# Reordering the seam between two batches of an attention and expert kernel, and a seven step reciprocal square root

## The chip, the core and the metric

The kernel runs on one core of a Trainium2 chip. The metric is device time in microseconds (us), the median of several runs; a profiled execution of the same program gives the trace from which all rows below are taken. TensorE does the matrix products, VectorE, ScalarE and GpSimd the element work, and SyncE issues the transfers.

## The reference

The input is 8 sequences of 512 tokens, 256 features wide. Each goes through an attention block and an expert block:

```python
q, k, v = x @ Wq.T, x @ Wk.T, x @ Wv.T          # 32 heads of 8, rope on q and k
kmean = mean of k over chunks of 32 tokens
gate = einsum('bshd,bnhd->bhsn', q, kmean)      # future chunks out, own chunk in
sel = top 4 chunks of gate per token and head
p = softmax(where(allowed by sel and causal, q @ k.T / sqrt(8), -1e30))
o = p @ v
o = o * rsqrt(mean(o * o) + 1e-6) * o_norm_weight * sigmoid(x @ Wg1.T @ Wg2.T)
x = layernorm(x + o @ Wo.T)
# experts: 2 shared, 16 routed of width 176, top 4 of sigmoid(x @ centroids.T) + bias
x = layernorm(x + x + shared(x) + sum over experts of gate_e * (relu(x @ w1_e + b1_e) @ w2_e + b2_e))
```

## The kernel before, in words

The order of the work is written out by hand, one program for each engine, with semaphores between them. There are no planners; a step waits only where the code says so, and every engine works its list in order.

The work is pipelined over batches. Turn `b` does the attention of batch `b` and, woven between its steps on every engine, the experts of batch `m = b - 1`. The expert columns are cut into 25 chunks `c` of up to 128: `up` is the first product of a chunk (6 matmuls in 3 parts), then ScalarE's `relu` and `high`, GpSimd's `low` (the rest that half precision leaves), and `down`, the second product (12 matmuls). Tensors with a high and a low half-precision part stand for one 32-bit tensor.

A turn has these stages:

- Top-k: `stack` transposes keys and queries on TensorE; VectorE picks the chunks (`best`, `select`).
- Maxima: 40 `max_unit` products, each followed by a reduction on VectorE (L1314).
- Softmax: 8 groups of 4 heads. `key_unit` products (L498), ScalarE's exponentials (L973), GpSimd's causal masks (L1072, a burst of three for each group), and the products with `v` (`outputs`, L704). VectorE's `copy_outputs` (L1334) empties the product's bank, TensorE's `to_tokens` (L714) transposes it, and VectorE's `keep` (L1339) takes it back. Each two groups are normalised in `two_groups`: squares, sum, `root_guess` (a shift and a subtraction on the bits), three Newton steps of three instructions (L1140 to L1142), the product. After the first Newton step of such a pair stands the `copy_outputs` of the next group.
- Seam: the last group goes to tokens and through `two_groups`, `heads_out` and `project_out` (L753, L760) give the attention's output, `layernorm` makes `x1n`. Between these TensorE projects the next batch (`project_v` L395, `project_qk` L401) and ScalarE turns it (`turned`, the rope's products). Then the new turn starts: `rank_rows` (L416), `transpose_q` (L424), `chunk_means` (L432) for the first half of the tokens, `x1_transpose` (L507) once `x1n` is there, the second half, `router` (L518), the second `chunk_means`, `up` of chunk 0 (L552), `chunk_gates` (L443), `gate_rows` (L526, L529), `up` of chunk 1, `open_outputs` (L538), the first `down` (L564).

On VectorE the seam is the layernorm, the rope of the second half, `x1T_parts` (L1161, the low part of the transposed `x1n`), `route` (L1166 to L1185) with `block_diagonal` (L1221) in its middle, then `best`. `chunk_gates` on TensorE waits for `block_diagonal`, `gate_rows` waits for the end of `route`. On ScalarE it is `x1T_parts` (L846), `stack_high` of tile 2 (L870), the router's exponential (L850), the two copies of `qT` (L905), `stack_high` of tile 3. GpSimd's four products of the same tiles (L1045) follow `stack_high`, then `low` of chunk 0 (L1029).

## Time and profile before

| What | us |
|---|---|
| median of 3 runs | 1563.69 (1562.2 to 1566.65) |
| profiled execution, device time | 1564.33 |
| profiled execution, span | 1562.6 |
| TensorE busy | 1387.1 (89%) |
| VectorE busy | 1180.3 (76%) |
| ScalarE busy | 846.1 (54%) |
| GpSimd busy | 539.8 (35%) |
| mean granted clock of TensorE, share of full speed | 0.932 |

A turn takes some 184 us, and there are seven seams between turns. The seam after the fourth turn lies at 715 to 757 us of the span; the rows below are mostly from there. A timeline row gives start, duration, engine, line, operation, output and input, count, and in brackets the idle time before it with what ended it. PE is TensorE's matmul queue, DVE VectorE, ACT ScalarE, POOL GpSimd.

### The profile page before, as it was taken

To read this page: it belongs to the slowest core of one execution; us is meant where nothing else is said; L and a number is where in the kernel's file an instruction comes from. 1 tells how busy PE (TensorE), PEld (TensorE's weight loads), DVE (VectorE), ACT (ScalarE), POOL (GpSimd) and SP (SyncE) were. 2 spreads that over 40 slices of the span, in tenths; PEclk is the share of its full clock that TensorE was granted. 3 is DMA by queue.
4 is the path that set the end of the run, shared out by engine and by line. 5 is a ranking of instruction groups with operands and counts; after the bars stand their busy time and mean duration, and the time that the engine had idled before them with its cause. 6 is when DMAs were issued, how large, how long until landed. Compare 5 with 4: busy or idle time off the path is not lost.

```text
span 1562.6 us, 29670 instructions
## 1 busy us (share of the span) xinstructions
PE 1387.1 (89%) x11024; PEld 755.2 (48%) x11024; DVE 1180.3 (76%) x3027; ACT 846.1 (54%) x1266; POOL 539.8 (35%) x638
## 2 busy tenths in 40 slices
PE   5588899898998989989999899989899899999697
PEld 3322575435643466434654257544664346542364
DVE  7994778867786778967788777876789677885634
ACT  5408663385725765276642957348562776428221
POOL 4204432254323542244422543235322443224143
PEclk8758899998999989999999989999899999998799
DMA  6000021100221012111221002210112101220031
GB/s 239 8 15 8 28 76 64 39 29 29 76 68 35 15 56 75 48 29 29 69 68 43 19 24 82 68 30 28 49 62 68 29 15 61 71 48 15 14 103 60
DMA packets 52212, 77.83 MB, mean 50 GB/s; under 512 B 6322, under 2 KB 26724, under 8 KB 51812
## 3 DMA queue, kind: packets, MB, share of 16 engines
q1 hardware_dynamic: 52068, 75.94, 16.4%
q8 instruction: 87, 1.43, 0.4%
q14 instruction: 57, 0.47, 0.1%
HBM read 67.00 MB, written 8.65 MB: 48 GB/s over the span
## 4 chain that ended last, share of the span: by engine, by line
PE 52%; DVE 19%; issue 10%; ACT 9%; POOL 5%; DVEq 3%; DMA 1%; POOLq 1%; SPq 0%
PE PS L564 12%; PE PS L552 10%; PE PS L704 7%; POOL hp L1029 5%; PE PS L481 4%; DVE CM L1314 4%; ACT UQ L973 3%; PE PS L498 3%; ACT hp L834 3%; DVE hr L1125 2%; PE PS L714 2%; PE PS L760 2%; ACT UK L973 2%; PE PS L401 2%; PE PS L451 2%
## 5 line engine op out<-in xcount | busy, mean ns | idle before, releaser
L1029 POOL TENSOR_TENSOR hp<-hr,hp 128x512 f16<-128x512 f32 (+1 forms) x200 | 234.8, 1174 | 637.0 <-ACT hp L834 605.1
L1314 DVE TENSOR_REDUCE CM<-PS 128x32 f32<-128x1024 f32 x320 | 382.1, 1220 | 47.6 <-PE PS L481 45.1
L564 PE MATMUL PS<-W,hp 128*128 128x256 f16 (+1 forms) x2400 | 322.2, 278 | 26.5 <-POOL hp L1029 23.9
L552 PE MATMUL PS<-x1T,W 128*128 128x512 f16 (+1 forms) x1200 | 315.1, 390 | 0.0
L564 PEld LDWEIGHTS PS<-W,hp 128*128 128x128 f16 (+1 forms) x2400 | 216.4, 99 | 124.4 <-POOL hp L1029 65.0
L825 ACT ACTIVATE hr<-PS,CF 128x512 f32<-128x512 f32 (+1 forms) x200 | 137.3, 686 | 207.4 <-PE PS L552 195.8
L834 ACT ACTIVATE hp<-hr 128x512 f16<-128x512 f32 (+1 forms) x178 | 112.5, 632 | 227.7 <-DVE hr L1125 226.0
L1125 DVE TENSOR_TENSOR hr<-hr,gB 128x512 f32<-128x512 f32 x176 | 121.1, 688 | 84.5 <-ACT hr L825 81.2
L973 ACT ACTIVATE UK<-PS 128x1024 f32<-128x1024 f32 x160 | 152.8, 1036 | 29.0 <-PE PS L498 28.0
L552 PEld LDWEIGHTS PS<-x1T,W 128*128 128x128 f16 (+1 forms) x1200 | 108.8, 101 | 114.9 <-issue 39.7
L973 ACT ACTIVATE UQ<-PS 128x1024 f32<-128x1024 f32 x160 | 151.8, 1044 | 5.2 <-PE PS L498 3.4
L498 PE MATMUL PS<-qET,kz 64*128 64x512 f16 (+3 forms) x1024 | 114.6, 311 | 27.6 <-ACT UK L973 20.4
L1072 POOL TENSOR_SCALAR_AFFINE_SELECT UK<-UK 128x512 f32<-128x512 f32 x128 | 78.3, 636 | 165.8 <-ACT UK L973 165.8
L481 PE MATMUL PS<-kz,qET 64*128 64x512 f16 (+3 forms) x1024 | 132.2, 318 | 0.0
L498 PEld LDWEIGHTS PS<-qET,kz 64*128 64x128 f16 x1024 | 32.3, 95 | 174.8 <-ACT UK L973 78.9
L1072 POOL TENSOR_SCALAR_AFFINE_SELECT UQ<-UQ 128x512 f32<-128x512 f32 x128 | 79.2, 641 | 65.2 <-ACT UQ L973 65.2
L704 PE MATMUL PS<-UK,vst 128*9 128x512 f32 (+3 forms) x1024 | 94.5, 466 | 0.0
L704 PE MATMUL PS<-UQ,vst 128*9 128x512 f32 (+3 forms) x1024 | 83.9, 434 | 0.0
L1334 DVE COPY ropeb<-PS 128x512 f32<-128x512 f32 x64 | 44.2, 690 | 49.3 <-PE PS L704 47.3
L883 ACT ACTIVATE UK<-PS,CF 128x128 f32<-128x128 f32 x112 | 55.9, 511 | 44.4 <-PE PS L401 44.4
L1045 POOL TENSOR_TENSOR UQ<-UK,UQ 128x512 f16<-128x512 f32 x32 | 40.5, 1266 | 100.1 <-ACT UQ L870 99.9
L919 ACT ACTIVATE kz<-PS 128x1024 f16<-128x1024 f16 x64 | 65.2, 1018 | 14.0 <-PE PS L451 14.0
(151 smaller groups left out, 1959.4 us busy)
## 6 DMA issues: line engine op xcount, KB each, us to landing
gB<-gates SPq DMA_DIRECT2D x64, 256.0 KB, 3.2
gB<-gates SPq DMA_DIRECT2D x32, 224.0 KB, 2.8
gB<-gates SPq DMA_DIRECT2D x32, 192.0 KB, 2.8
gB<-gates SPq DMA_DIRECT2D x32, 160.0 KB, 2.5
xT<-in_xT SPq DMA_DIRECT2D x8, 512.0 KB, 3.7
qET<-rows SPq DMA_DIRECT2D x16, 256.0 KB, 5.8
v<-in_x SPq DMA_DIRECT2D x8, 512.0 KB, 4.1
gB<-gates SPq DMA_DIRECT2D x32, 128.0 KB, 2.8
```

The costliest lines, as they stand in the source:

```text
L481: mm = pe.matmul(PS[:, r + half, o:o + w], qET[rows, a, t * P:(t + 1) * P], kz[rows, a, 0:w], start=False, stop=True, skip_group_check=Tru ...
L498: mm = pe.matmul(PS[:, r + half, o:o + w], kz[rows, a, t * P:(t + 1) * P], qET[rows, a, t * P:S], start=True, stop=True, tile_position=(64 ...
L552: mm = pe.matmul(PS[0:w, BK_H[c % 2], :], W1[:, a, k, bass.ds(f0, w)], x1T[:, e, k, :], start=(n == 0), stop=(n == 5))
L564: mm = pe.matmul(PS[:, BK_Y + j // 2, (j % 2) * D:(j % 2 + 1) * D], hp[0:w, slot, a, j * P:(j + 1) * P], W2[0:w, e, bass.ds(c, 1), :].rear ...
L704: mm = pe.matmul(PS[32 * hh:32 * hh + HD + 1, BK_PV, t * P:S], vst[:, gs % 2, t, hh, :], PT[gs % 2][:, hh, o:o + w], start=(n == 0), stop= ...
L825: nc.scalar.activation(hr[0:w, slot, :], PS[0:w, BK_H[c % 2], :], ACT.Relu, bias=bias).then_inc(act_h, 1)
L834: nc.scalar.activation(hp[0:w, slot, 0, :], hr[0:w, slot, :], ACT.Copy).then_inc(s_high, 1)
L973: nc.scalar.activation(dst, src, ACT.Exp, scale=SCALE).then_inc(act_p, 1)
L1029: nc.gpsimd.tensor_tensor(hp[0:w, slot, 1, :], hr[0:w, slot, :], hp[0:w, slot, 0, :], ALU.subtract).then_inc(pool_hp, 1)
L1072: nc.gpsimd.affine_select(block, block, [[0, HG], [1, P]], ALU.is_ge, zero, base=0, channel_multiplier=-1).then_inc(pool_p, 1)
L1125: nc.vector.tensor_tensor(hr[:, slot, :], hr[:, slot, :], gB[:, r, :], ALU.mult).then_inc(dve_h, 1)
L1314: nc.vector.tensor_reduce(dst, src, AX.X, ALU.max).then_inc(dve_cm, 1)
```

## The change

There are six edits.

1. Roots: `newton(n, 3)` (nine instructions) becomes `refine` (four) and `newton` (three). The constant by which `refine` leaves the result off is folded into a scalar of the instructions before and after. In `two_groups` the four of `refine` now stand ahead of `copy_outputs`, where three stood.
2. At the end of a turn, TensorE does `project_v` of tile 1 where `project_qk` of tile 0 stood, then the last `to_tokens`, then `project_qk` of tile 0. `project_v` of tile 1 is gone from its later place.
3. Sixteen products of constants, `spare`, stand ahead of `x1_transpose`. They write columns of bank 0 that nothing reads before they are overwritten.
4. The second `chunk_means` stands ahead of `router`, and on VectorE `block_diagonal` ahead of `route`.
5. On ScalarE the copies of `qT` stand ahead of the router's exponential, and `stack_high` of tile 2 behind it.
6. `up` of chunk 1 stands ahead of `gate_rows`.

On TensorE, the start of the turn of batch 1, from the last projection to `open_outputs`; L507 is `x1_transpose`, L518 the router, L432 the means, L443 the chunk gates, L526 and L529 the gate rows. Before:

```order
L401 MATMUL PS<-WA,xT 128x512 x4
L416 MATMUL PS<-xT,WA 8x256 x4
L424 MATMUL PS<-CF,UK 128x128 x4
L432 MATMUL PS<-CF,UK 128x4 x4
L507 MATMUL PS<-CF,x1n 128x128 x8
L424 MATMUL PS<-CF,UK 128x128 x4
L518 MATMUL PS<-CENT,x1T 128x16 x24
L432 MATMUL PS<-CF,UK 128x4 x4
L552 MATMUL PS<-x1T,W 128x512 x6
L443 MATMUL PS<-ropeb,qT 128x256 x6
L526 MATMUL PS<-CF,er 16x128 x4
L529 MATMUL PS<-CH,gsp 34x128 x4
```

The same place now:

```order
L422 MATMUL PS<-xT,WA 8x256 x4
L430 MATMUL PS<-CF,UK 128x128 x4
L438 MATMUL PS<-CF,UK 128x4 x4
L414 MATMUL PS<-CG 128x256 x16
L513 MATMUL PS<-CF,x1n 128x128 x8
L430 MATMUL PS<-CF,UK 128x128 x4
L438 MATMUL PS<-CF,UK 128x4 x4
L524 MATMUL PS<-CENT,x1T 128x16 x24
L558 MATMUL PS<-x1T,W 128x512 x6
L449 MATMUL PS<-ropeb,qT 128x256 x6
L558 MATMUL PS<-x1T,W 128x512 x6
L532 MATMUL PS<-CF,er 16x128 x4
```

Sixteen products of `CG` have come in ahead of the transposes, the means have moved ahead of the router, and a second six of `up` ahead of the gate rows.

On VectorE, in `two_groups` of the softmax stage, from the guess of the root to the last root instruction; the COPY is `copy_outputs` of the next group. Before:

```order
L1135 TENSOR_SCALAR rep<-rep 128x32
L1140 TENSOR_TENSOR rep<-rep 128x32
L1141 SCALAR_TENSOR_TENSOR rep<-rep 128x32
L1142 SCALAR_TENSOR_TENSOR rep<-rep 128x32
L1334 COPY ropeb<-PS 128x512
L1140 TENSOR_TENSOR rep<-rep 128x32
L1141 SCALAR_TENSOR_TENSOR rep<-rep 128x32
L1142 SCALAR_TENSOR_TENSOR rep<-rep 128x32
```

Now:

```order
L1141 TENSOR_SCALAR rep<-rep 128x32
L1147 TENSOR_TENSOR rep<-rep 128x32
L1148 TENSOR_TENSOR rep<-rep 128x32
L1149 SCALAR_TENSOR_TENSOR rep<-rep 128x32
L1150 SCALAR_TENSOR_TENSOR rep<-rep 128x32
L1350 COPY ropeb<-PS 128x512
L1156 TENSOR_TENSOR rep<-rep 128x32
L1157 SCALAR_TENSOR_TENSOR rep<-rep 128x32
```

The copy has one root instruction more ahead of it, and three behind it instead of six.

On ScalarE, the same seam; L905 is the copy of `qT`, L850 the exponential, L870 `stack_high`. Before:

```order
L846 ACTIVATE x1T<-PS 128x512 x2
L870 ACTIVATE UQ<-UK 128x32x16
L870 ACTIVATE UK<-UK 128x32x2x8
L850 ACTIVATE er<-PS 128x64
L905 ACTIVATE qT<-PS 128x512 x2
```

Now:

```order
L853 ACTIVATE x1T<-PS 128x512 x2
L909 ACTIVATE qT<-PS 128x512 x2
L857 ACTIVATE er<-PS 128x64
L877 ACTIVATE UQ<-UK 128x32x16
L877 ACTIVATE UK<-UK 128x32x2x8
```

`stack_high` of tile 2, and with it GpSimd's work on the tile, now comes after the exponential.

```diff
@@ -164,7 +164,7 @@
         vst = sb("vst", [P, 2, NT, HG, HD + 1])
         repf = rep[:, :, :].rearrange("p h w -> p (h w)")
-        ms, ry, rt = (repf[:, n * NT * H:(n + 1) * NT * H] for n in range(3))
+        ms, ry, rt, rw = (repf[:, n * NT * H:(n + 1) * NT * H] for n in (0, 1, 2, 4))
         st6 = repf[:, 3 * NT * H:3 * NT * H + NT * 6].rearrange("p (t s) -> p t s", t=NT)
         mv = repf[:, 3 * NT * H + NT * 6:3 * NT * H + NT * 8].rearrange("p (t s) -> p t s", t=NT)
@@ -407,6 +407,12 @@
                     project_v(b, j)
                     project_qk(b, j)
+            def spare(bank, count):
+                for _ in range(count):
+                    pe.matmul(PS[:, bank, D:2 * D], identb, causal_q, start=True, stop=True)
             def rank_rows(b):
                 pe.wait_ge(act_v, 2 * b + 2)
@@ -574,21 +580,20 @@
                 transpose_q(b, 0, 2)
                 chunk_means(b, 0, 2)
                 if m is not None:
+                    spare(0, 16)
                     x1_transpose(m)
                 pe.wait_ge(dve_rope, (b + 1) * NT)
                 transpose_q(b, 2, NT)
+                chunk_means(b, 2, NT)
                 if m is not None:
                     router(m)
-                chunk_means(b, 2, NT)
-                if m is not None:
-                    up(m, 0, 0)
-                    up(m, 0, 1)
-                    up(m, 0, 2)
+                    for part in range(3):
+                        up(m, 0, part)
                 chunk_gates(b)
                 if m is not None:
-                    gate_rows(m)
                     for part in range(3):
                         up(m, 1, part)
+                    gate_rows(m)
                     open_outputs(m)
                     for j in range(NT):
                         down(m, 0, 0, j)
@@ -740,8 +745,10 @@
                     outputs(NG - 1, NG - 1, t)
                 if more:
                     pe.wait_ge(act_p, (b + 1) * TU + RING)
+                    project_v(b + 1, 1)
+                to_tokens(NG - 1)
+                if more:
                     project_qk(b + 1, 0)
-                to_tokens(NG - 1)
                 def heads_out(k):
@@ -764,7 +771,7 @@
                 heads_out(0)
                 if more:
-                    project(b + 1, 1, 2)
+                    project_qk(b + 1, 1)
                     project_v(b + 1, 2)
                 project_out(0)
                 heads_out(1)
@@ -897,13 +904,12 @@
                 nc.scalar.activation(g1T, PS[0:ROW_G1 + HD, BK_Y, 0:D], ACT.Copy).then_inc(act_g1, 1)
                 if m is not None:
                     x1T_parts(m)
-                stack_high(b, 2, 3)
-                if m is not None:
-                    route(m)
                 for k in range(KT):
                     act.wait_ge(pe_qT, b * KT + k + 1)
                     nc.scalar.activation(qT[:, k, :], PS[:, k, :], ACT.Copy).then_inc(act_qT, 1)
-                stack_high(b, 3, NT)
+                if m is not None:
+                    route(m)
+                stack_high(b, 2, NT)
                 if m is not None:
                     chunks(m, 0, 1)
                 if m is not None:
@@ -1134,12 +1140,22 @@
                 link(nc.vector.tensor_scalar(t.bitcast(I32), a.bitcast(I32), 1, None, ALU.logical_shift_right))
                 link(nc.vector.tensor_scalar(y.bitcast(I32), t.bitcast(I32), -1.0, float(ROOT), ALU.mult, ALU.add))
-            def newton(n, steps):
+            def refine(n):
+                a, y, t, w = (buf[:, 0:n] for buf in (ms, ry, rt, rw))
+                link(nc.vector.tensor_tensor(t, y, y, ALU.mult))
+                link(nc.vector.tensor_tensor(t, t, a, ALU.mult))
+                link(nc.vector.scalar_tensor_tensor(out=w, in0=t, scalar=-10.0 / 3.0, in1=t, op0=ALU.add, op1=ALU.mult))
+                link(nc.vector.scalar_tensor_tensor(out=y, in0=w, scalar=5.0, in1=y, op0=ALU.add, op1=ALU.mult))
+            def newton(n):
                 a, y, t = ms[:, 0:n], ry[:, 0:n], rt[:, 0:n]
-                for _ in range(steps):
-                    link(nc.vector.tensor_tensor(t, y, y, ALU.mult))
-                    link(nc.vector.scalar_tensor_tensor(out=t, in0=t, scalar=-0.5, in1=a, op0=ALU.mult, op1=ALU.mult))
-                    link(nc.vector.scalar_tensor_tensor(out=y, in0=t, scalar=1.5, in1=y, op0=ALU.add, op1=ALU.mult))
+                link(nc.vector.tensor_tensor(t, y, y, ALU.mult))
+                link(nc.vector.scalar_tensor_tensor(out=t, in0=t, scalar=-0.5 * 9.0 / 64.0, in1=a, op0=ALU.mult, op1=ALU.mult))
+                link(nc.vector.scalar_tensor_tensor(out=y, in0=t, scalar=1.5, in1=y, op0=ALU.add, op1=ALU.mult))
             def layernorm(src, dst, done):
                 for j in range(NT):
@@ -1148,9 +1164,10 @@
                 for j in range(NT):
                     nc.vector.bn_aggr(mv[:, j, :], st6[:, j, :])
                 dve.drain()
-                link(nc.vector.tensor_scalar(ms[:, 0:NT], mv[:, :, 1], 1e-5, None, ALU.add))
+                link(nc.vector.tensor_scalar(ms[:, 0:NT], mv[:, :, 1], 1e-5, 64.0 / 9.0, ALU.add, ALU.mult))
                 root_guess(NT)
-                newton(NT, 3)
+                refine(NT)
+                newton(NT)
                 for j in range(NT):
                     nc.vector.tensor_scalar(dst[:, j, :], src[:, j, :], mv[:, j, 0:1], ry[:, j:j + 1],
                                             ALU.subtract, ALU.mult).then_inc(done, 1)
@@ -1160,14 +1177,12 @@
                     dve.wait_ge(act_x1T, m * KT + k + 1)
                     nc.vector.tensor_tensor(x1T[:, 1, k, :], PS[:, 4 + k, :], x1T[:, 0, k, :], ALU.subtract).then_inc(dve_x1T, 1)
-            def route(m, b=None):
+            def route(m):
                 dve.wait_ge(act_rt, m + 1)
                 link(nc.vector.tensor_scalar(er[:, :, :], er[:, :, :], 1.0, None, ALU.add))
                 link(nc.vector.reciprocal(er[:, :, :], er[:, :, :]))
                 link(nc.vector.tensor_tensor(sc[:, :, 0:NE], er[:, :, :], rbias.unsqueeze(1).to_broadcast([P, NT, NE]), ALU.add))
-                if b is not None:
-                    block_diagonal(b)
                 for j in range(NT):
                     nc.vector.max(rtop[:, j, :], sc[:, j, 0:NE])
                 dve.drain()
@@ -1266,11 +1281,12 @@
                 rope(b, 2, NT)
                 if m is not None:
                     x1T_parts(m)
-                if m is not None:
-                    route(m, b)
+                if m is None:
+                    low_w2(0)
+                block_diagonal(b)
+                if m is not None:
+                    route(m)
                 else:
-                    low_w2(0)
-                    block_diagonal(b)
                     low_w2(1)
                     dve.wait_ge(act_w, 6)
                     nc.vector.tensor_tensor(CENT[:, 1], CENTF[:, :, :], CENT[:, 0], ALU.subtract).then_inc(dve_w, 1)
@@ -1357,11 +1373,11 @@
                     link(nc.vector.scalar_tensor_tensor(out=tok(ms), in0=tok(rt), scalar=HD * 1e-6, in1=tok(ms),
                                                         op0=ALU.mult, op1=ALU.add))
                     root_guess(NT * 2 * HG)
-                    newton(NT * 2 * HG, 1)
+                    refine(NT * 2 * HG)
                     if not last:
                         copy_outputs(i * 2 + 2)
-                    newton(NT * 2 * HG, 2)
-                    link(nc.vector.scalar_tensor_tensor(out=sq, in0=u8, scalar=0.5 * HD ** 0.5,
+                    newton(NT * 2 * HG)
+                    link(nc.vector.scalar_tensor_tensor(out=sq, in0=u8, scalar=0.5 * HD ** 0.5 * 3.0 / 8.0,
                                                         in1=tok(ry).unsqueeze(3).to_broadcast([P, NT, 2 * HG, HD]),
                                                         op0=ALU.mult, op1=ALU.mult))
                     eg_4 = eg_i.rearrange("p t (h d) -> p t h d", d=HD)
```

## Rows read from the trace of the kernel before

**Rows 1.** The page, the chain that ended last, by engine.
```profile
PE 52%; DVE 19%; issue 10%; ACT 9%; POOL 5%; DVEq 3%; DMA 1%; POOLq 1%; SPq 0%
```

**Rows 2.** Timeline of TensorE in the softmax stage, 705 to 707 us.
```profile
706.60 0.66 PE L714 MATMUL PS<-CF,ropeb 128*128 128x128 f32 x4
```

**Rows 3.** Timeline of VectorE, the same stretch.
```profile
705.25 0.53 DVE L1142 SCALAR_TENSOR_TENSOR rep<-rep 128x32 f32<-128x32 f32 x1
705.85 0.69 DVE L1334 COPY ropeb<-PS 128x512 f32<-128x512 f32 x1
```

**Rows 4.** Timeline of GpSimd, the same stretch.
```profile
705.10 1.81 POOL L1072 TENSOR_SCALAR_AFFINE_SELECT UQ<-UQ 128x512 f32<-128x512 f32 x3 [1.19 <-ACT UQ L973]
```

**Rows 5.** Timeline of VectorE, then TensorE, same stage of another turn.
```profile
328.23 0.69 DVE L1334 COPY ropeb<-PS 128x512 f32<-128x512 f32 x1
...
328.98 0.66 PE L714 MATMUL PS<-CF,ropeb 128*128 128x128 f32 x4 [0.61 <-DVE ropeb L1334]
```

**Rows 6.** Timeline of TensorE, the seam after the fourth turn.
```profile
720.79 0.60 PE L714 MATMUL PS<-CF,ropeb 128*128 128x128 f32 x4
...
739.06 1.97 PE L507 MATMUL PS<-CF,x1n 128*128 128x128 f32 x8 [2.38 <-DVE x1n L1155]
...
742.64 0.74 PE L518 MATMUL PS<-CENT,x1T 128*128 128x16 f16 x24 [0.76 <-DVE x1T L1161]
...
747.43 2.83 PE L443 MATMUL PS<-ropeb,qT 128*128 128x256 f32 x12 [1.84 <-DVE ropeb L1221]
750.55 0.60 PE L526 MATMUL PS<-CF,er 128*16 128x128 f32 x4 [0.30 <-DVE gsp L1185]
...
751.42 1.47 PE L552 MATMUL PS<-x1T,W 128*128 128x512 f16 x6
752.82 1.04 PE L538 MATMUL PS<-GR 34*128 34x256 f16 x8
```

**Rows 7.** Timeline of VectorE, the same seam.
```profile
719.11 0.68 DVE L1334 COPY ropeb<-PS 128x512 f32<-128x512 f32 x1
721.42 0.31 DVE L1339 COPY CM<-PS 128x144 f32<-128x144 f32 x1 [1.63 <-PE PS L714]
...
724.96 0.19 DVE L1140 TENSOR_TENSOR rep<-rep 128x32 f32<-128x32 f32 x1
...
735.49 0.16 DVE L1140 TENSOR_TENSOR rep<-rep 128x4 f32<-128x4 f32 x1
...
743.67 0.90 DVE L1166 TENSOR_SCALAR er<-er 128x64 f32<-128x64 f32 x1 [1.29 <-ACT er L850]
...
745.28 1.18 DVE L1168 TENSOR_TENSOR sc<-er,CF 128x64 f32<-128x64 f32 x1
746.53 0.76 DVE L1221 TENSOR_TENSOR ropeb<-PS,CF 128x256 f32<-128x256 f32 x2
...
750.27 0.23 DVE L1185 TENSOR_TENSOR gsp<-er,gsp 128x64 f16<-128x64 f32 x1
```

**Rows 8.** Timeline of GpSimd, the same seam.
```profile
742.26 1.15 POOL L1045 TENSOR_TENSOR UQ<-UK,UQ 128x512 f16<-128x512 f32 x1 [7.12 <-ACT UQ L870]
...
747.44 1.16 POOL L1029 TENSOR_TENSOR hp<-hr,hp 128x512 f16<-128x512 f32 x1
```

**Rows 9.** Busy time by engine, granted clock (PEclk) after the five engines.
```profile
739.00:741.00 2.00, 1.94 (x9) 1.94 (x10) 1.60 (x6) 0.60 (x1) 0.00 (x0) 0.53 0.01 3
745.00:747.00 2.00, 0.59 (x3) 0.09 (x1) 1.85 (x4) 1.94 (x4) 1.89 (x3) 1.00 0.00 0
```

**Rows 10.** Timeline of TensorE, the first and the seventh seam.
```profile
187.15 1.97 PE L507 MATMUL PS<-CF,x1n 128*128 128x128 f32 x8 [2.70 <-DVE x1n L1155]
...
199.62 0.61 PE L526 MATMUL PS<-CF,er 128*16 128x128 f32 x4 [0.83 <-DVE gsp L1185]
...
1290.58 1.09 PE L507 MATMUL PS<-CF,x1n 128*128 128x128 f32 x8 [2.38 <-DVE x1n L1155]
...
1301.31 0.60 PE L526 MATMUL PS<-CF,er 128*16 128x128 f32 x4
```

## The prediction, made before the changed kernel ran

> **What bounds the kernel now.** I read the chain of waits first. TensorE has 52% of it and VectorE 19% [rows 1], so most of the span is TensorE's own work, and the rest is handed over to VectorE somewhere. The timelines of the engines side by side show where. Two places matter for this change.
>
> In the softmax stage TensorE's `to_tokens` (L714) starts right behind VectorE's `copy_outputs`: the copy ends at 706.54, L714 starts at 706.60 [rows 2, 3]. The copy itself stands behind a root instruction that took 0.53 where its like takes 0.19 [rows 3, 7], and it ended about when the first of GpSimd's three masks did: the burst runs from 705.10 for 1.81, so its parts end near 705.7, 706.3 and 706.9 [rows 4]. That is, a VectorE instruction with two operands in SBUF stands still while GpSimd runs one.
>
> At the seam the chain is serial: last `to_tokens`, `two_groups`, output projection, layernorm, `x1_transpose`, router, `route`, `gate_rows`. TensorE idles 2.38 ahead of `x1_transpose`, 1.84 ahead of the chunk gates, 0.30 ahead of the gate rows [rows 6]. From `gate_rows` on it is busy without a break into the top-k stage, so what `gate_rows` gains the turn gains.
>
> **The seam, step by step.** T0 is the start of `x1_transpose`, 739.06 in the fourth seam [rows 6].
>
> Ahead of T0. The last `copy_outputs` ends at 719.79 [rows 7], but L714 starts at 720.79 [rows 6], behind `project_qk` of tile 0. With `project_v` there, half the columns, it can start at about 719.84: 0.95 earlier, and `keep` (721.42 now) with it. `two_groups` then has two steps fewer, each 0.19 plus 0.07 between two instructions (705.78 to 705.85 [rows 3, 7]): 0.5. ScalarE gets tile 0 some 1.1 later, yet is still done with tile 1 about when the second half of the heads is ready, so I cost that at nothing; if the cover is gone it costs 0.3. Together 1.5. The layernorm has two steps fewer at 0.16 plus 0.08 [rows 7]: 0.5. T0 comes 2.0 earlier. The fillers, 16 products of 256 columns, need about 1.7 (estimate: `up` does six of 512 columns in 1.47 with its end [rows 6], so a column costs 0.42 ns and a product 0.11) and lie in the 2.38 of idle.
>
> From T0 to the gate rows. Now this takes 11.49 in the fourth seam, 12.47 in the first and 10.73 in the seventh [rows 6, 10]. The spread comes from the granted clock: at 739 to 741 it is 0.53, the lower level of 1.2 GHz for most of it, right after the 2.38 of idle [rows 9], and `x1_transpose` takes 1.97 where it takes 1.09 at 2.4 GHz [rows 6, 10]. With the fillers the idle is gone and I take 1.09 everywhere. The router then starts at T0 + 3.1 instead of 3.58 (742.64); the means fit ahead of it, since it waits for `x1T` anyhow. If the clock were low they would not fit. `route` starts 1.03 behind the router's start, as now (743.67 against 742.64), at T0 + 4.1, without `block_diagonal` (0.76) in it.
>
> But `stack_high` of tile 2 has moved behind the exponential. GpSimd's work on the tiles, which runs from 742.26 to the end of `low` at 748.60 [rows 8], T0 + 3.2 to T0 + 9.5, will run from T0 + 4.7 to T0 + 11.0, over all of `route`. Now only the first three instructions of `route` meet it: L1166 takes 0.90 and L1168 1.18, their likes 0.2 [rows 7]. Moved, L1168, the scalar step, the division and the split of the gates meet it too. Unhindered, `route` would take 4.4 (6.83 now from 743.67 to 750.50, less 0.76 of the diagonal and its gap, less some 1.6 of these stalls). Four or five stalls of 0.5 to 0.9 put its end at T0 + 11.2. Gate rows at T0 + 11.3, against a mean near 11.9 over the seams: gain 0.6. Bounds: 2.6 without a stall, when TensorE's own work (router, `up`, gates, `up`) ends at T0 + 9.1; a loss of 0.5 with one stall more.
>
> Here the trace and a rule of the Trainium skill can be laid side by side. SBUF — State Buffer, section "SBUF: two separate sides", says that a GpSimd instruction and a VectorE one with two SBUF inputs lock each other out for a whole instruction, and that only a GpSimd instruction that reads SBUF does this to the latter kind. The masks and tile products in this trace agree (0.53 against 0.19). By the second half of the rule the zeroing of `EQ` and `EK`, which reads nothing, would leave the earlier `two_groups` alone, and the seam would gain 0.2 more; nothing above rests on it.
>
> Behind the gate rows. `open_outputs` starts 2.27 behind them (752.82 against 750.55), because `up` of chunk 1 lies between [rows 6]. With `up` done before, it waits only for ScalarE's two copies, some 1.8: gain 0.5. The transfer of the gates leaves earlier by as much as the gate rows do. VectorE, done with `route`, follows TensorE through top-k and has waits there, so it doesn't take the 0.5 back.
>
> Per seam 2.0 + 0.6 + 0.5 = 3.1, over seven seams 21.7. The last batch adds the shorter roots on its serial path: 0.5 in `two_groups`, 0.5 in each of two layernorms, 1.5.
>
> **What the same edits cost.** First, the copy. `refine` puts four instructions ahead of `copy_outputs` instead of three. The first three end as now, the third at 705.78 with the first mask; the fourth, from 705.85, meets the second mask and ends near 706.37. The copy starts at 706.43 instead of 705.85: 0.58 later. L714 has no slack. A row of another turn shows what follows: there the copy ran from 328.23 and TensorE stood idle 0.61 before L714 [rows 5]. ScalarE gets its scores later by as much and the period is longer by it. This happens at three of the four pairs of each turn, 24 times: 13.9. Bounds: 0, if the instruction slips in between two masks, and 15 with one stall after another; I take 13.9 since the rows leave no gap between the masks.
>
> Second, the clock behind the new gap. TensorE will have nothing from T0 + 9.1 to T0 + 11.3, 2.2 of idle, then 0.9 more ahead of `open_outputs`. Idle of 2.38 ahead of T0 was followed by the lower level in all seven seams; idle of 1.84 at 745.4 to 747.4 was not, the clock stood at 1.00 [rows 6, 9]. 2.2 lies between. The work behind the gap is dense, so a stretch of 3.4 at half speed (the low one in the fourth seam lasted from 739.1 to 742.5) costs 1.7. I take two seams of seven: 3.4. Bounds: 0, and 12 to 20 if all seven fall, some for twice as long.
>
> **The sum.** 1564.33 - 21.7 - 1.5 + 13.9 + 3.4 = 1558.4. The median of the runs shown lies 0.6 below the profiled execution, so 1557.8, say 1558. With other places for stalls in `route`, the likeliest case's own range is 1552 to 1563.
>
> **The rivals.** A: the clock falls behind the gate rows at every seam. For it: 2.2 is nearer to 2.38 than to 1.84 and a second idle follows. Against it: the work ahead of the gap is dense, where ahead of T0 it was small products. Time: 1554.4 (the sum without the 3.4) + 7 x 1.7 = 1566 for one stretch each, up to 1574 for longer ones, 1568 in the middle, slower than before. It decides the sign from about 9.3 us of clock loss on, five or six seams.
>
> B: the copy isn't late, because the fourth instruction finds its way. Then 1558 - 13.9 = 1544. Against it: all 24 third instructions ended with a GpSimd instruction, none slipped in.
>
> C: the change does little: GpSimd's work, shifted by 1.5, holds `route` longer and `gate_rows` stands where it did against T0, and the 0.6 turns into a loss of 0.5. Time: 1558 + 7 x 1.1 = 1566, 1562 with one half of it. For it: five of the instructions of `route` lie in GpSimd's stretch. Against it: each can wait for one GpSimd instruction only, at most 1.15.
>
> D: no stalls in `route` beyond today's: 1558 - 7 x 2.0 = 1544.
>
> **How the numbers follow.** My case 0.38, A 0.26, B 0.12, C 0.14, D 0.10. A change under 0.3% (4.7 us) is about what a measurement of this kernel can't tell from none; faster means under 1559.0. My case lies on both sides of that line, 0.27 faster and 0.11 same. B and D are faster, 0.22. C gives 0.03 faster, 0.07 same and 0.04 slower. A gives 0.03 same and 0.23 slower. Faster 0.52, same 0.21, slower 0.27. The range for 8 in 10 is 1542 to 1571.
>
> **What the profile will show.** L714 behind an even group's copy starts about 1.3 behind the third root instruction's end instead of 0.8, with about 0.6 of idle ascribed to VectorE, 24 times. `keep` of the last group starts 0.95 earlier behind the copy. `x1_transpose` takes 1.1 in every seam. From T0 to the gate rows it is 11.3, with the long instructions of `route` ending where GpSimd's end. The granted clock behind the gate rows tells between my case and A. I am wrong if the softmax stage keeps its pace, if the gate rows come at T0 + 9, or if the clock there is low in most seams.

## The result, and the profile after

The changed kernel takes 1574.94 us (1573.22 to 1576.44, five runs) against 1563.69 (1562.2 to 1566.65, five runs beside them). The ratio is 1.0069, with a 95% interval of 1.0056 to 1.0081: slower by 0.7%, above the forecast's range and of the other sign. The profiled execution took 1574.94 with a span of 1572.9; the one before 1564.33 with 1562.6.

The page of the changed kernel: the chain of waits by engine, and busy time by engine. This answers to [rows 1].

```profile
PE 50%; DVE 24%; issue 10%; ACT 7%; POOL 5%; DVEq 3%; POOLq 1%; DMA 0%; SPq 0%; ACTq 0%
PE 1400.4 (89%) x11136; PEld 761.0 (48%) x11136; DVE 1165.3 (74%) x2931; ACT 845.4 (54%) x1266; POOL 537.5 (34%) x638
```

VectorE does 15.0 less (1180.3 before) and yet has more of the chain, 24% against 19%. TensorE is busy 13.3 longer (1387.1 before). The fillers by themselves take 13.3. `down` takes 12.8 more (335.0 against 322.2) and `open_outputs` 3.8 more, since they run at a lower clock, as will be seen; the other products take that much less, most of it the small ones at the seam.

The softmax stage on VectorE, at the fourth turn. This answers to [rows 3, 5].

```profile
709.96 0.52 DVE L1149 SCALAR_TENSOR_TENSOR rep<-rep 128x32 f32<-128x32 f32 x1
710.55 0.51 DVE L1150 SCALAR_TENSOR_TENSOR rep<-rep 128x32 f32<-128x32 f32 x1
711.14 0.69 DVE L1350 COPY ropeb<-PS 128x512 f32<-128x512 f32 x1
```

GpSimd's masks beside it, answering to [rows 4]:

```profile
709.80 1.81 POOL L1078 TENSOR_SCALAR_AFFINE_SELECT UQ<-UQ 128x512 f32<-128x512 f32 x3 [1.19 <-ACT UQ L979]
```

And TensorE there, answering to [rows 2]:

```profile
711.89 0.66 PE L719 MATMUL PS<-CF,ropeb 128*128 128x128 f32 x4 [0.57 <-DVE ropeb L1350]
```

Read them together: the third root instruction ends about when the first mask does (710.48), the fourth about when the second does (711.06), and only then does the copy run. TensorE stands idle 0.57 for it, so rival B, a copy that isn't late, is out. The view of waits has this over the whole span (total us, times, the longest): 25 times, 0.66 each on average. 24 of them stand behind `refine`; the other is the last group of the last batch, which waited in the kernel before too.

```profile
PE PS L719 <- DVE ropeb L1350: 16.5, 25, 1.7
PE PS L532 <- DVE gsp L1200: 11.9, 8, 2.3
```

The second row is the gap ahead of the gate rows. Its seven seams are not alike: TensorE waits 2.27 there in four of them (the first, second, fourth and fifth) and 0.58 in the other three. TensorE at the fourth seam, answering to [rows 6]: L760 `heads_out`, L767 `project_out`, L414 the fillers, L513 `x1_transpose`, L532 the gate rows, L544 `open_outputs`, L570 `down`, L558 `up`.

```profile
730.99 1.95 PE L767 MATMUL PS<-WO,qET 128*128 128x256 f32 x8
732.77 0.60 PE L760 MATMUL PS<-CF,qT 128*128 128x128 f32 x4
...
741.69 1.91 PE L414 MATMUL PS<-CG 128*128 128x256 bf16 x16
743.74 1.09 PE L513 MATMUL PS<-CF,x1n 128*128 128x128 f32 x8
...
751.33 1.46 PE L558 MATMUL PS<-x1T,W 128*128 128x512 f16 x6
755.05 0.60 PE L532 MATMUL PS<-CF,er 128*16 128x128 f32 x4 [2.26 <-DVE gsp L1200]
...
756.90 1.66 PE L544 MATMUL PS<-GR 34*128 34x256 f16 x8 [0.92 <-ACT GR L866]
758.49 2.74 PE L570 MATMUL PS<-W,hp 128*128 128x256 f16 x12
```

`x1_transpose` now takes 1.09, as forecast, and the gate rows start 11.31 behind it (755.05 - 743.74), where 11.3 was forecast. Behind them 12 products of `down` take 2.74. Windows of the same seam, whose columns are stretch, its length, then busy time and count of TensorE, its weight loads, VectorE, ScalarE and GpSimd, the granted clock, the DMA share and GB/s, answering to [rows 9]:

```profile
757.00:759.00 2.00, 2.00 (x11) 1.18 (x10) 1.85 (x15) 0.95 (x2) 0.94 (x1) 0.54 0.10 27
759.00:761.00 2.00, 2.00 (x11) 1.44 (x10) 1.65 (x4) 0.00 (x0) 0.24 (x1) 0.50 0.67 203
763.00:765.00 2.00, 2.00 (x14) 1.35 (x13) 1.57 (x17) 1.14 (x2) 0.00 (x0) 0.76 0.16 54
```

Right behind the gap the clock drops to 0.50, the lower level of 1.2 GHz, for nearly 7 us in which TensorE is never idle. In the third, sixth and seventh seam it goes another way. At the third, `up` of chunk 0 and the gate rows are:

```profile
562.48 2.65 PE L558 MATMUL PS<-x1T,W 128*128 128x512 f16 x6
...
570.09 0.60 PE L532 MATMUL PS<-CF,er 128*16 128x128 f32 x4 [0.58 <-DVE gsp L1200]
```

The clock is at 1.2 GHz here for 3.4 us ahead of the gate rows already, from 3.8 behind the start of `x1_transpose`, though TensorE had no long idle before. That slows six products of `up` to 2.65 and eats up most of the wait, so it costs nothing: the gate rows start 11.31 to 11.34 behind `x1_transpose` in all seven seams. Behind them the clock falls a second time, for 3.4 us. What brought on the earlier fall is not shown.

So the low clock hasn't gone. Before, it lay over the transposes and what follows them, up to the gate rows, and part of it was hidden by waits. Now a stretch of it lies behind the gate rows, in dense work, where nothing hides it.

The start times of named products cut both spans into the same stretches. These are the differences, summed over all turns (the last `to_tokens` counts from its last product):

| Stretch | before | after | difference |
|---|---|---|---|
| to the first key product | 123.89 | 124.18 | +0.29 |
| first key product to first `to_tokens`, 8 | 88.97 | 87.70 | -1.27 |
| first to last `to_tokens`, 8 | 271.59 | 276.21 | +4.62 |
| last `to_tokens` to `x1_transpose`, 8 | 145.33 | 140.01 | -5.32 |
| `x1_transpose` to gate rows, 7 | 83.7 | 79.2 | -4.45 |
| gate rows to first top-k `stack`, 7 | 59.25 | 73.06 | +13.81 |
| last batch, gate rows to last `down` | 66.16 | 69.38 | +3.22 |
| top-k, maxima and the end | | | -0.65 |
| sum | | | +10.3 |

One row stands out: +13.81 behind the gate rows.

### The profile page after: what moved, and what is told of

Read it like the earlier page. It is cut to its first block, busy times and chain, and to the rows that moved or that the text cites. A ratio compares the mean times of both kernels' runs of the same rounds, so it can differ in the third digit from the quotient of the medians.

```text
span 1572.9 us, 29702 instructions
## 1 busy us (share of the span) xinstructions
PE 1400.4 (89%) x11136; PEld 761.0 (48%) x11136; DVE 1165.3 (74%) x2931; ACT 845.4 (54%) x1266; POOL 537.5 (34%) x638
## 3 DMA queue, kind: packets, MB, share of 16 engines
q8 instruction: 88, 1.44, 0.4%
## 4 chain that ended last, share of the span: by engine, by line
PE 50%; DVE 24%; issue 10%; ACT 7%; POOL 5%; DVEq 3%; POOLq 1%; DMA 0%; SPq 0%; ACTq 0%
PE PS L570 13%; PE PS L558 9%; PE PS L709 6%; POOL hp L1035 5%; PE PS L487 4%; DVE CM L1330 4%; PE PS L719 3%; PE PS L504 2%; ACT hp L841 2%; ACT UK L979 2%; DVE hr L1131 2%; PE PS L767 2%; DVE ropeb L1350 2%; PE PS L401 2%; PE PS L457 2%
## 5 line engine op out<-in xcount | busy, mean ns | idle before, releaser
L570 PE MATMUL PS<-W,hp 128*128 128x256 f16 (+1 forms) x2400 | 335.0, 285 | 23.7 <-POOL hp L1035 21.2
L558 PE MATMUL PS<-x1T,W 128*128 128x512 f16 (+1 forms) x1200 | 317.2, 392 | 0.0
L570 PEld LDWEIGHTS PS<-W,hp 128*128 128x128 f16 (+1 forms) x2400 | 222.7, 102 | 128.9 <-POOL hp L1035 62.2
L558 PEld LDWEIGHTS PS<-x1T,W 128*128 128x128 f16 (+1 forms) x1200 | 110.2, 102 | 116.7 <-issue 41.4
```

Source lines behind the costliest of these rows:

```text
L558: mm = pe.matmul(PS[0:w, BK_H[c % 2], :], W1[:, a, k, bass.ds(f0, w)], x1T[:, e, k, :], start=(n == 0), stop=(n == 5))
L570: mm = pe.matmul(PS[:, BK_Y + j // 2, (j % 2) * D:(j % 2 + 1) * D], hp[0:w, slot, a, j * P:(j + 1) * P], W2[0:w, e, bass.ds(c, 1), :].rear ...
```

## The experiments

All ratios are against the kernel before, run on the same chip, with the 95% interval. A stretch "per seam" is a mean over the seven.

### Fillers in the new gap

```diff
                         up(m, 1, part)
+                    spare(2, 18)
                     gate_rows(m)
```

> The changed kernel with one edit: 18 more products of the constants, into a bank that is free there, between up of chunk 1 and the gate rows, where TensorE idles 2.26. Theory (the clock behind the gate rows is the largest loss): the granted clock stays at 2.4 GHz behind the gate rows in all seven seams, the way from the gate rows to the first stack goes from a mean of 10.44 to about 8.1, and the time from 1575 to about 1558. Rival (the stretch is long for another reason, say the order of GpSimd's work, and the low clock only sits on it): the clock may stay high but the stack comes where it did, 1575; if the fillers come late themselves, more.

Measured 1556.11, ratio 0.9957 [0.9943, 0.9971]. Nothing but 18 unused products was added, and it is 18.8 faster than the changed kernel. TensorE at the fourth seam:

```profile
745.74 2.13 PE L414 MATMUL PS<-CG 128*128 128x256 bf16 x18
748.18 0.60 PE L532 MATMUL PS<-CF,er 128*16 128x128 f32 x4 [0.31 <-DVE gsp L1201]
...
750.99 1.49 PE L570 MATMUL PS<-W,hp 128*128 128x256 f16 x12
```

and its windows:

```profile
750.00:752.00 2.00, 1.97 (x18) 1.59 (x19) 1.85 (x17) 1.09 (x2) 0.81 (x1) 1.00 0.08 18
```

The same `down` takes 1.49 instead of 2.74, and the clock stays at 1.00. From the gate rows to the first `stack` it is 8.03 in all seven seams, against a mean of 10.44. That is 73.06 - 56.2 = 16.9 of clock loss in the changed kernel. The low stretches ahead of the gate rows are gone too, though the fillers stand behind them; why is not shown. The last batch, gate rows to last `down`, took 66.16 here, 3.2 less, though nothing was put there. This too is the clock. In the changed kernel it is low for 6.8 us right behind the last gate rows:

```profile
1494.00:1501.00 7.00, 6.45 (x24) 3.69 (x25) 0.00 (x0) 1.09 (x2) 0.29 (x1) 0.53 0.50 148
```

Here and in the kernel before it is not low there at all.

### The copy one instruction earlier

`refine` issues `copy_outputs` between its third and fourth instruction, in the place it had before.

```diff
-                    refine(NT * 2 * HG)
-                    if not last:
-                        copy_outputs(i * 2 + 2)
+                    refine(NT * 2 * HG, None if last else lambda: copy_outputs(i * 2 + 2), 3)
```

> The changed kernel with one edit: in two_groups the copy of the next group's outputs stands behind the third of the four instructions of refine, as it stood behind three before the change. Theory (the copy is 0.6 late three times a turn): the way from the first to_tokens to the last goes from 34.5 to about 32.7 a turn, 24 x 0.6 = 14 in all, time about 1561. Rival (ScalarE's exponentials bound that stage, the late copy costs nothing): 1575.

Measured 1562.99, ratio 0.9997 [0.9988, 1.0007]. The stretch from first to last `to_tokens` falls from 276.21 to 262.49, by 13.7. The late copy costs the changed kernel in that stretch what was forecast for it. The time fell by 12.0. The clock behind the gate rows is still low in all seven seams (10.81 to the first `stack`).

### Both

The two edits above together.

> The changed kernel with both edits, the fillers ahead of the gate rows and the copy behind three instructions. Theory: the two losses lie in different stages and add, 1575 - 17 - 14 = 1544. Rival (one of them is hidden behind the other, or the stage that gains gives it back in the maxima stage): about 1558.

Measured 1546.6, ratio 0.9882 [0.9860, 0.9904]. The two losses are separate and nearly add: 18.8 and 12.0 alone, 28.3 together. One of the seven seams still shows a low stretch (9.66, the others 8.03).

### The roots alone

The kernel before with edit 1 only: `refine` and `newton`, with the copy behind all four, nothing moved at the seam.

```diff
-                    newton(NT * 2 * HG, 1)
+                    refine(NT * 2 * HG)
...
-                    newton(NT * 2 * HG, 2)
+                    newton(NT * 2 * HG)
```

> The kernel before with the first edit alone: seven root instructions instead of nine, four of them ahead of the copy. Theory: 14 lost in the softmax stage, some 1.0 gained ahead of each x1_transpose (7) and 1.5 in the last batch, net about 1569. Rival (the copy is harmless): 1555.

Measured 1563.5, ratio 0.9995 [0.9975, 1.0015], between the two, and too wide (1554.77 to 1568.19) to choose by time; the mean granted clock goes with it, 0.950 in the shortest run and 0.933 in the longest. The stretches choose. First to last `to_tokens` is 282.28, 10.7 more than before, and the last `to_tokens` to `x1_transpose` is 17.09 per seam, 0.99 less than the 18.08 of before. TensorE's rows of this kernel:

```profile
714.40 0.65 PE L714 MATMUL PS<-CF,ropeb 128*128 128x128 f32 x4 [0.60 <-DVE ropeb L1345]
...
736.35 1.09 PE L507 MATMUL PS<-CF,x1n 128*128 128x128 f32 x8 [1.91 <-DVE x1n L1166]
```

So the shorter roots bring the 1.0 a seam that was forecast and pay for it with the late copies. It is 10.7 and not 13.9 because in the kernel before five of its 24 copies were late already.

### The tile's stack ahead of the exponential again

Edit 5 undone: ScalarE's `stack_high` of tile 2 first, then the exponential, then the copies of `qT`.

```diff
+                stack_high(b, 2, 3)
+                if m is not None:
+                    route(m)
                 for k in range(KT):
...
-                if m is not None:
-                    route(m)
-                stack_high(b, 2, NT)
+                stack_high(b, 3, NT)
```

> The changed kernel with edit 5 undone alone: ScalarE does stack_high of tile 2 ahead of the router's exponential and the copies of qT behind it, as before. Theory: GpSimd's tile work starts some 2 earlier against T0, route meets it in fewer instructions, the gate rows come at T0 + 10.0 instead of 11.3, TensorE's idle ahead of them falls from 2.26 to about 1.0, and with that the granted clock stays high behind them: gate rows to first stack 8.0 instead of 10.4. Time 1575 - 7 x 1.3 - 7 x 2.4 = 1549. Rival (the end of route isn't set by GpSimd's work): gate rows at T0 + 11.3, clock low, 1575.

Measured 1556.21, ratio 0.9957 [0.9942, 0.9972]: 18.7 faster than the changed kernel, though 7 short of the forecast. GpSimd's rows in the changed kernel:

```profile
748.45 1.16 POOL L1051 TENSOR_TENSOR UQ<-UK,UQ 128x512 f16<-128x512 f32 x1 [8.16 <-ACT UQ L877]
...
751.27 1.15 POOL L1051 TENSOR_TENSOR UQ<-UK,UQ 128x512 f16<-128x512 f32 x1
...
753.50 1.15 POOL L1035 TENSOR_TENSOR hp<-hr,hp 128x512 f16<-128x512 f32 x1
```

VectorE's `route` beside them, also in the changed kernel:

```profile
747.88 0.20 DVE L1183 TENSOR_SCALAR er<-er 128x64 f32<-128x64 f32 x1 [0.38 <-ACT er L857]
748.78 0.91 DVE L1185 TENSOR_TENSOR sc<-er,CF 128x64 f32<-128x64 f32 x1
...
751.78 0.67 DVE L1196 TENSOR_SCALAR gsum<-gsum 128x4 f32<-128x4 f32 x1
...
752.78 0.84 DVE L1198 TENSOR_TENSOR er<-er,gsum 128x64 f32<-128x64 f32 x1
753.69 1.01 DVE L1199 CAST gsp<-er 128x64 f16<-128x64 f32 x1
754.77 0.23 DVE L1200 TENSOR_TENSOR gsp<-er,gsp 128x64 f16<-128x64 f32 x1
```

Four of them take 0.67 to 1.01 where undisturbed ones of such sizes take 0.20 and 0.23. What they lose together, some 2.6, is about the 2.26 that TensorE waits. Two of the four, L1196 and L1199, read a single tensor, so it isn't instructions with two operands alone that are held. TensorE with edit 5 undone:

```profile
746.04 0.60 PE L532 MATMUL PS<-CF,er 128*16 128x128 f32 x4 [0.98 <-DVE gsp L1201]
...
748.97 2.74 PE L570 MATMUL PS<-W,hp 128*128 128x256 f16 x12
```

GpSimd is through sooner, the gate rows start 10.27 to 10.57 behind `x1_transpose` instead of 11.3, and the idle is 0.98 instead of 2.26. (That is in four seams. In the other three a low stretch slows TensorE ahead of the gate rows, they come at 10.57 without any idle, and the clock isn't low behind them.) In three of the four seams with the idle of 0.98, this one among them, the clock still falls, which I had not allowed for: 1.6 each, five of the seven that were missing. The gate rows came 0.9 a seam earlier and not 1.3, which is the rest.

### The same with the copy behind the second instruction

> The kernel of e5_stack_first with the copy of the next group's outputs behind the second instruction of refine. Theory: what the two undo adds; the copy starts before the first mask of the burst and TensorE never waits for it, to_tokens to to_tokens 32.5 or less a turn. Time about 1549 - 15 = 1534. Rival (the instructions now behind the copy meet more masks and the pair ends too late for the next copy): 1540 or more.

Measured 1542.24, ratio 0.9865 [0.9844, 0.9885], 8 short of the forecast, again for three low seams (11.3 to the first `stack` in each, 3.3 over the 8.03 of the rest, 10 in all). The softmax stretch, 258.87, is 3.6 shorter than with the copy behind the third instruction.

### No fillers

```diff
                 if m is not None:
-                    spare(0, 16)
                     x1_transpose(m)
```

> The changed kernel without edit 3, the 16 products ahead of x1_transpose. Theory: the lower clock comes at T0 again and x1_transpose takes 1.97 instead of 1.09, the router comes 0.5 to 1.5 later, since the means now stand ahead of it at half speed; T0 to the gate rows 12 to 13; the low stretch may end before the gate rows or be prolonged by the idle there. Time 1575 + 7 x 1 = 1582, less if the low stretch behind the gate rows is gone with it (then 1570). Rival (the fillers do nothing for the clock): 1575.

Measured 1581.34, ratio 1.0117 [1.0102, 1.0132], the time that was forecast, though not step by step. TensorE:

```profile
745.74 1.09 PE L513 MATMUL PS<-CF,x1n 128*128 128x128 f32 x8 [1.91 <-DVE x1n L1171]
...
750.38 2.72 PE L558 MATMUL PS<-x1T,W 128*128 128x512 f16 x6
...
761.07 2.74 PE L570 MATMUL PS<-W,hp 128*128 128x256 f16 x12
```

Without them the clock falls around `x1_transpose` in all seven seams, but mostly not in time for it: it takes 1.97 in two of them, 1.44 and 1.70 in two and 1.09 in three, this one among them, where 1.97 was forecast. The work between it and the gate rows is slowed (2.72 for six products of `up`), and the clock is low behind them too. `x1_transpose` to gate rows takes 12.15 per seam instead of 11.32, 5.8 over seven, of the 6.4 measured. Edit 3 helps; it is one gap short.

### Fewer fillers

The kernel with both, with 8 products in the gap in place of 18.

> The kernel of e3_both with 8 products ahead of the gate rows instead of 18, so that 1.3 of idle is left there and 0.9 ahead of open_outputs. Theory (an idle of 1.3 doesn't bring the lower clock, as the 1.84 of the fourth seam of before didn't): 1546, as e3_both. Rival (what counts is that TensorE is fed without a break): low clock in all seams, 1561.

Measured 1550.43, ratio 0.9896 [0.9857, 0.9935], between the two theories. 1.40 of idle is left, and in the profiled execution the clock falls in three of seven seams. That execution was the slowest of four, 1559.7; the others took 1540.08 to 1553.44, at a mean granted clock of 0.957 to 0.945 against its 0.939. By that clock, the same kernel spends more or less time at 1.2 GHz from one execution to the next.

### The best version

Edit 5 undone, the copy behind the second instruction, and fillers on both sides of the gate rows.

```diff
+                    spare(2, 8)
                     gate_rows(m)
+                    spare(2, 7)
                     open_outputs(m)
```

> The kernel of e6_stack_first_copy_2 with 8 products ahead of the gate rows and 7 ahead of open_outputs, into the two idle stretches of 1.0 and 0.9. Theory: the clock stays at 2.4 GHz behind the gate rows in all seams, gate rows to first stack 8.03 each (9.44 in the mean without), the gate rows stay at T0 + 10.3; time 1542 - 10 = 1532. Rival (the fillers themselves hold up the gate rows or open_outputs): first stack later than 8.3, no gain over 1542.

Measured 1535.22, ratio 0.9826 [0.9808, 0.9844]. TensorE is idle for 0.1 at most ahead of the gate rows and of `open_outputs`:

```profile
731.30 1.04 PE L414 MATMUL PS<-CG 128*128 128x256 bf16 x8
732.43 0.60 PE L532 MATMUL PS<-CF,er 128*16 128x128 f32 x4
...
733.30 0.94 PE L414 MATMUL PS<-CG 128*128 128x256 bf16 x7
734.28 1.03 PE L544 MATMUL PS<-GR 34*128 34x256 f16 x8
```

It is 8.03 from the gate rows to the first `stack` in all seven seams. In the softmax stage VectorE shows how the copy stands behind the second root instruction:

```profile
689.58 0.19 DVE L1155 TENSOR_TENSOR rep<-rep 128x32 f32<-128x32 f32 x1
...
690.19 0.69 DVE L1361 COPY ropeb<-PS 128x512 f32<-128x512 f32 x1 [0.42 <-PE PS L711]
691.05 0.49 DVE L1161 SCALAR_TENSOR_TENSOR rep<-rep 128x32 f32<-128x32 f32 x1
```

VectorE waits 0.42 for the product here, so the copy is as early as it can be. The instruction held by a mask (0.49 against 0.19) now comes behind it.

### The best version without edit 2

`project_qk` of tile 0 stands ahead of the last `to_tokens` again.

> The kernel of e9_best with edit 2 undone alone: project_qk of tile 0 ahead of the last to_tokens again, project_v of tile 1 later. Theory: from e4_roots_alone against the changed kernel, edit 2 moved the last to_tokens 0.9 forward and x1_transpose only 0.3; so this is 0.3 x 7 = 2 slower than e9_best. Rival (my forecast of 0.95 and nothing lost behind it): 7 slower.

Measured 1534.59, ratio 0.9815 [0.9801, 0.9829]: no difference that the runs can show, and 2 is too little for them. The last `to_tokens` comes 0.85 earlier with edit 2 (the softmax stretches, 258.85 against 264.81, over seven), but `x1_transpose` then comes 17.65 behind it instead of 17.07. TensorE's rows without edit 2, last `to_tokens` and the second `heads_out`:

```profile
708.86 0.60 PE L721 MATMUL PS<-CF,ropeb 128*128 128x128 f32 x4
...
715.13 0.63 PE L760 MATMUL PS<-CF,qT 128*128 128x128 f32 x4
```

and with it, where `heads_out` is L762:

```profile
704.25 0.60 PE L721 MATMUL PS<-CF,ropeb 128*128 128x128 f32 x4
...
711.21 0.60 PE L762 MATMUL PS<-CF,qT 128*128 128x128 f32 x4
```

6.27 against 6.96: most of what the earlier `to_tokens` gains is lost ahead of `heads_out`. What is left, 0.27 a seam, is the 0.3 of the theory.

## Why the prediction was wrong

The profiled execution came out at 1574.94 where the sum gave 1558.4, a miss of 16.5. In the spans, term by term (the spans differ by 10.3, the device times by 10.6):

| Term | forecast | measured |
|---|---|---|
| behind the gate rows, clock included | -0.1 | +13.8 |
| `x1_transpose` earlier, seven seams | -14.0 | -9.1 |
| last batch | -1.5 | +0.9 |
| late copies | +13.9 | +10.7 |
| `x1_transpose` to gate rows | -4.2 | -4.45 |
| the rest | 0 | -1.6 |

**The step that failed** is the second of what the edits cost: "I take two seams of seven: 3.4." The clock fell in all seven and cost 16.9, of which 0.43 x 7 = 3.0 comes back by the shorter wait for `open_outputs` (8.46 to 8.03). So rival A held, and above the middle of its price. Both factors of the term were too small. The clock fell in seven seams and not in two. And one seam cost 1.6 (three seams), 2.7 (two) or 3.3 (two) and not 1.7, since the low stretch lasted 6.8 us in the four seams with the long wait and 3.4 in the others. I had read its length off the fourth seam of before [rows 9], the shortest: in the kernel before it was 3.4 there, 6.8 in the seventh seam and 10.2 in the other five. This is the first seam's window, clock 0.51 over 10.5 us:

```profile
186.00:196.50 10.50, 8.59 (x53) 6.36 (x54) 8.19 (x27) 5.12 (x10) 5.11 (x5) 0.51 0.02 5
```

I had put the gap right (2.2, measured 2.27 in four seams) and named the idle of 0.9 behind it, but weighed it against two cases of before, 2.38 and 1.84 [rows 6], and let the dense work ahead of it count in its favour. The filler experiment shows the cause: it fills the idle and changes nothing else in the program.

**Ahead of `x1_transpose`** the forecast was 2.0 a seam, and it was 1.3. The roots gave 0.99 as forecast. Edit 2 gave 0.3 instead of 0.95. This was the edit whose cover I had costed at nothing, on ScalarE, where I should have followed TensorE's own order. In the changed kernel VectorE has the second half of the heads ready here:

```profile
731.29 0.42 DVE L1384 SCALAR_TENSOR_TENSOR qT<-qT,CM 128x256 f32<-128x256 f32 x1
```

It ends at 731.71, while the second L760 starts at 732.77, behind `project_out` of the first half, which runs from 730.99. TensorE's list, and not the heads, sets that time. The best version without edit 2 agrees: no difference in time.

**The late copies** were right in mechanism and size: 13.7 by the experiment that moves the copy back. As a difference from before they count 10.7, since five copies there were late already; I had seen one of them [rows 5] and taken it as an example of the price, not as a part of the old time.

**From `x1_transpose` to the gate rows** the time held: 1.09 with the fillers, 11.3 to the gate rows, and the stalls in `route` where GpSimd works. The low stretches there in three seams were not forecast and cost nothing. Rival C, a route held longer than that, is out; so is D. The rule of the Trainium skill weighed there (SBUF — State Buffer, section "SBUF: two separate sides") can now be looked at with a row of after. First VectorE, an instruction with two operands in SBUF:

```profile
726.85 0.42 DVE L1370 TENSOR_TENSOR CM<-CM 128x256 f32<-128x256 f32 x1
```

and GpSimd beside it, filling a buffer with a constant (that of `EK` isn't zero, as I had called it):

```profile
726.75 0.95 POOL L1042 MEMSET UK<- 128x1024 f32 x1
```

In the kernel before, the same instruction met one of GpSimd's that reads a buffer:

```profile
721.82 0.86 DVE L1354 TENSOR_TENSOR CM<-CM 128x256 f32<-128x256 f32 x1
721.80 0.62 POOL L1039 TENSOR_SCALAR UK<-CH 128x512 f16<-128x512 f16 x1
```

0.42 is what this instruction takes undisturbed. Beside the constant it took that in all seven seams, and beside the reading instruction 0.86 in all seven. The trace agrees with the rule.

**The last batch** lost 0.9 where I had it gain 1.5. `x1_transpose` came 2.34 earlier there, more than the 1.0 of the shorter roots; the clock is low for most of that stretch before (12.4 us of 19.1) and for 8.7 us of 16.8 now, so what the roots gave there can't be told apart from what the clock did. The work behind the gate rows took 3.2 longer, and that is the clock again. Over all the kernels run this part took 66.15 or 66.16 where the clock was never low in it (three kernels), 67.8 where it was low for 3.4 us (four), 69.4 or 69.5 for 6.8 us (four) and 70.09 for 9.5 us (one). Why it falls there in one kernel and not in another stays open: it doesn't go with the idle ahead of the last gate rows, which was 1.2 to 1.7 where the clock stayed high and 0.7 to 3.0 where it fell. With this the clock took 16.9 + 3.2 = 20.1 where I had put 3.4.

## What to carry to other kernels

When an edit moves work from behind a wait to ahead of it, the wait is still there and TensorE now sits idle in it. Read the granted clock of the dense work behind that gap first, and put products on a free bank into the gap. And read the length of a low stretch at more than one place: here it was 3.4, 6.8 or 10.2 us in one and the same kernel. A small VectorE instruction of a serial chain can cost up to a whole GpSimd instruction if one that reads SBUF runs beside it (0.53 against 0.19, 0.91 against 0.23 here). So a consumer's copy goes ahead of the first such instruction, and GpSimd's bulk is started where the serial chain isn't.

## What the runs showed of the hardware

Less idle time on TensorE was followed by the lower clock than I had expected from the trace of before. The table goes by seams, over the changed kernel and all its variants. It has the idle time ahead of the gate rows. Ahead of `open_outputs` TensorE then waited another 0.8 to 0.9, but for the last row. "Low" is a stretch at 1.2 GHz behind the gate rows.

| Idle ahead of the gate rows | kernels | seams | low |
|---|---|---|---|
| 2.27 | changed kernel 4, copy earlier 7, no fillers 2 | 13 | 13 |
| 1.40 | 8 fillers | 7 | 3 |
| 0.98 | edit 5 undone 4, and with the copy behind the second 5 | 9 | 6 |
| 0.35 to 1.03, low stretch shortly ahead | changed kernel 3, no fillers 5 | 8 | 8 |
| none, low stretch shortly ahead | edit 5 undone 3, and with the copy behind the second 2 | 5 | 0 |
| 0.31 | 18 fillers 7, both 7 | 14 | 1 |
| 0.1, and none ahead of `open_outputs` | best 7, best without edit 2 7 | 14 | 0 |

The idle ahead of `open_outputs` alone was thus not followed by a low stretch in any of five seams. It was never taken away alone, so what it adds to the other is open, and so is why seams with the same idle differ. A low seam cost 1.6 to 3.3 (9.65 to 11.33 to the first `stack` against 8.03). `down`'s 12 products took 2.74 at 1.2 GHz and 1.49 at 2.4 GHz. So 18 products that compute nothing, 2.1 us of TensorE's time a seam, made the kernel 18.8 faster.
